# Pairing the PV quads: two quads of heads at a time in slots 0 and 8 of an attention and FFN pipeline

## What is computed

```python
def layer(x, ctx):
    q = layernorm(x) @ w_q.T                  # (8, 256, 128), 16 heads of 8
    k, v = ctx @ w_k.T, ctx @ w_v.T
    s = einsum('bhtd,bhsd->bhts', q, k) / sqrt(8)
    attn = softmax(where(mask, s, -inf), axis=-1)
    x = x + einsum('bhts,bhsd->bhtd', attn, v) @ w_o.T
    n = layernorm(x)
    h = silu(n @ (w_gate / 127).T) * (n @ (w_up / 127).T)
    return x + h @ (w_down / 127).T
```

## Time and profile before

| | us |
|---|---|
| median of 3 runs | 187.32 |
| lowest, highest | 187.08, 190.01 |
| the profiled execution | 189.59 |
| its span | 187.8 |

### The profile page before, as it was taken

The page is one execution under the profiler, slowest core; times in us unless marked ns, Lnnn a source line. Parts: engine busy times, 40 slices in busy tenths (PEclk is TensorE's granted clock), DMA queues, the critical chain, the costliest instruction groups (busy, mean ns, idle before and its releaser), DMA issues.

```text
span 187.8 us, 4293 instructions
## 1 busy us (share of the span) xinstructions
PE 168.6 (90%) x1636; PEld 105.9 (56%) x1636; DVE 133.3 (71%) x308; ACT 107.2 (57%) x226; POOL 67.0 (36%) x114
## 2 busy tenths in 40 slices
PE   5858998599996999999999999998999999997883
PEld 4648554254452556557656655754565466655863
DVE  6853897676799578968896886899689815425441
ACT  5432014657794488577867785777577577533030
POOL 6233605918427533950674085004100500310100
PEclk9996999659999699999999999999999999999999
DMA  4739797491096029405930870394000000000100
GB/s 147 261 97 183 210 179 231 134 185 24 8 245 94 3 63 213 68 0 155 173 47 12 232 133 0 93 212 67 3 30 2 3 2 28 5 28 0 31 2 28
DMA packets 17381, 17.06 MB, mean 91 GB/s; under 512 B 1520, under 2 KB 15984, under 8 KB 16688
## 3 DMA queue, kind: packets, MB, share of 16 engines
q1 hardware_dynamic: 16896, 16.12, 37.4%
q10 hardware_dynamic: 464, 0.67, 1.3%
HBM read 9.24 MB, written 7.34 MB: 88 GB/s over the span
## 4 chain that ended last, share of the span: by engine, by line
PE 54%; DVE 17%; issue 15%; POOL 6%; ACT 3%; DMA 2%; ACTq 1%; SPq 1%; POOLq 0%
PE pv_bank L336 12%; PE score_bank L276 9%; DVE neg_max L742 9%; PE pv_bank L403 5%; PE max_bank L293 4%; PE ffn_bank L389 4%; PE ffn_bank L377 3%; DMA ctx_all<-ctxT 2%; PE ffn_bank L380 2%; PE prep_bank L315 2%; PE prep_bank L307 2%; PE post_bank L365 2%; PE post_bank L352 2%; DVE stats L811 1%; PE prep_bank L311 1%
## 5 line engine op out<-in xcount | busy, mean ns | idle before, releaser
L742 DVE TENSOR_REDUCE neg_max<-max_bank 128x2 f32<-128x512 f32 x128 | 82.0, 685 | 17.9 <-PE max_bank L293 17.3
L566 ACT ACTIVATE probs<-score_bank 128x512 f32<-128x512 f32 x128 | 70.0, 597 | 20.7 <-PE score_bank L276 20.7
L293 PE MATMUL max_bank<-k_ops,q_ops 49*128 49x256 bf16 x256 | 44.0, 280 | 2.8 <-DVE neg_max L742 2.8
L276 PE MATMUL score_bank<-q_ops,k_ops 51*128 51x256 bf16 x256 | 43.7, 280 | 1.9 <-ACT probs L566 1.1
L336 PE MATMUL pv_bank<-probs,v_ops 128*32 128x256 f32 x512 | 35.2, 390 | 0.0
L276 PEld LDWEIGHTS score_bank<-q_ops,k_ops 51*128 51x128 bf16 x256 | 19.8, 95 | 22.1 <-ACT probs L566 9.9
L293 PEld LDWEIGHTS max_bank<-k_ops,q_ops 49*128 49x128 bf16 x256 | 17.4, 95 | 8.3 <-DVE neg_max L742 5.6
L990 POOL CAST max_parts<-neg_max 128x16 bf16<-128x16 f32 x14 | 2.8, 198 | 51.7 <-DVE neg_max L742 51.7
L336 PEld LDWEIGHTS pv_bank<-probs,v_ops 128*32 128x32 f32 x512 | 14.7, 110 | 11.2 <-issue 5.4
L403 PE MATMUL pv_bank<-ident_bf 128*128 128x128 bf16 x212 | 18.5, 242 | 1.9 <-POOL ident_bf L1020 1.9
L403 PEld LDWEIGHTS pv_bank<-ident_bf 128*128 128x128 bf16 x212 | 15.0, 110 | 5.9 <-issue 3.6
(11 more groups left out here) (117 smaller groups left out, 221.0 us busy)
## 6 DMA issues: line engine op xcount, KB each, us to landing
k_ops<-k_rows SPq DMA_DIRECT2D x7, 384.0 KB, 4.8
q_ops<-q_rows SPq DMA_DIRECT2D x7, 384.0 KB, 6.1
k_rows<-kq_parts SPq DMA_DIRECT2D x8, 192.0 KB, 2.1
q_rows<-kq_parts SPq DMA_DIRECT2D x8, 192.0 KB, 2.2
k_rows<-kq_parts SPq DMA_DIRECT2D x8, 128.0 KB, 2.1
q_rows<-kq_parts SPq DMA_DIRECT2D x8, 128.0 KB, 2.1
out<-y SPq DMA_DIRECT2D x8, 128.0 KB, 2.1
x_all<-x SPq DMA_DIRECT2D x1, 768.0 KB, 6.6
```

The source lines that it names most:

```text
L276: mm = pe.matmul(score_bank[k % 2][:, t * S:(t + 1) * S], rows(k_ops, b, ROWS)[:, k, t * P:(t + 1) * P], rows(q_ops, b, ROWS)[:, k, :], st ...
L293: mm = pe.matmul(max_bank[k % 2][:, t * S:(t + 1) * S], rows(q_ops, b, MAX_ROWS)[:, k, t * P:(t + 1) * P], rows(k_ops, b, MAX_ROWS)[:, k, ...
L566: act.activation(probs[:, k % RING].rearrange("p t s -> p (t s)"), score_bank[k % 2][:, :], ACT.Exp, scale=SCALE).then_inc(probs_ready, 1)
L742: dve.tensor_reduce(neg_max[:, b % 2, :, k], max_bank[k % 2][:, :].rearrange("p (t s) -> p t s", t=TT), AX.X, ALU.max, negate=True).then_i ...
```

## The change

The two quads 2 and 3 of batch b - 1 stand together in slot 0, and quads 0 and 1 of batch b in slot 8, each pair with nothing else in its slot. `turn_xn2` and `turn_max(b, 1)` go from slot 0 to slot 2, ahead of `turn_xn1` and `project_down`; `project_attn` and `turn_max(b + 1, 0)` from slot 8 to slot 10, in that order; gate and up of chunk 1 from slot 10 to slot 12, ahead of `project_v`; chunk 2 stays alone in slot 14. Step 7 is changed in its slots 0 and 2 only. ScalarE's and VectorE's orders follow: `copy_pv` stands behind exp 1, `copy_xn2_t` and `copy_max_t(b, 1)` behind exp 3, `copy_max_t(b + 1, 0)` behind exp 11, the tanh of chunk 1 behind exp 13, `residual` and `stats_of_x1` behind head_max 11, `moments_of_x1` and `eps_of_x1` behind head_max 13. No instruction is added or removed; GpSimd's and SyncE's orders stay.

```diff
@@ TensorE, the steps
                 both(b, 0)
+                if b >= 1:
+                    times_v(b - 1, 2)
+                    times_v(b - 1, 3)
+                both(b, 2)
                 if b >= 2:
                     turn_xn2(b - 2)
...
                 turn_max(b, 1, prep_bank)
-                if b >= 1:
-                    times_v(b - 1, 3)
-                both(b, 2)
...
                 times_v(b, 0)
+                times_v(b, 1)
+                both(b, 10)
+                if b >= 1:
+                    project_attn(b - 1)
                 if prep:
                     pe.wait_ge(kq_copied, b + 2)
                 else:
                     pe.wait_ge(max_t_ready, 2 * b + 2)
                 turn_max(b + 1, 0, prep_bank)
-                if b >= 1:
-                    project_attn(b - 1)
-                both(b, 10)
+                both(b, 12)
                 if b >= 2:
                     pe.wait_ge(hidden_done, CH * (b - 2) + 1)
                     project_gate_up(b - 2, 1, ffn_bank)
-                both(b, 12)
-                times_v(b, 1)
...
                     project_gate_up(b - 2, 2, ffn_bank)
-                times_v(b, 2)
 
             b = LAST
             both(b, 0)
+            times_v(b - 1, 2)
+            times_v(b - 1, 3)
+            both(b, 2)
             turn_xn2(b - 2)
             pe.wait_ge(max_t_ready, 2 * b + 1)
             turn_max(b, 1, prep_bank)
-            times_v(b - 1, 3)
-            both(b, 2)
@@ ScalarE, the steps (the same three moves stand in step 7)
                 exp(b, 0)
                 exp(b, 1)
+                if b >= 1:
+                    copy_pv(b - 1)
+                exp(b, 2)
+                exp(b, 3)
                 if b >= 2:
                     copy_xn2_t(b - 2)
                 copy_max_t(b, 1, prep_bank)
-                exp(b, 2)
-                exp(b, 3)
-                if b >= 1:
-                    copy_pv(b - 1)
-                else:
+                if b == 0:
                     place_v(2, prep_bank)
...
-                exp(b, 8)
-                exp(b, 9)
+                for k in range(8, 12):
+                    exp(b, k)
                 copy_max_t(b + 1, 0, prep_bank)
-                exp(b, 10)
-                exp(b, 11)
+                exp(b, 12)
+                exp(b, 13)
                 if b >= 2:
                     gate_tanh(b - 2, 1, ffn_bank)
-                exp(b, 12)
-                exp(b, 13)
@@ VectorE, the steps
-                head_max(b + 1, 8)
-                head_max(b + 1, 9)
+                for k in range(8, 12):
+                    head_max(b + 1, k)
                 if b >= 1:
                     residual(b - 1)
                     stats_of_x1(b - 1)
-                head_max(b + 1, 10)
-                head_max(b + 1, 11)
+                head_max(b + 1, 12)
+                head_max(b + 1, 13)
                 if b >= 1:
                     moments_of_x1(b - 1)
                     eps_of_x1(b - 1)
-                head_max(b + 1, 12)
-                head_max(b + 1, 13)
                 if b >= 2:
                     hide(b - 2, 1, ffn_bank)
```

## The result

| us | before | changed |
|---|---|---|
| median | 187.85 (4 executions) | 195.22 (4) |
| lowest, highest | 187.08, 190.01 | 194.6, 196.11 |
| the profiled execution | 189.59 | 194.6 |
| its span | 187.8 | 192.8 |
| granted clock, mean over the span | 0.964 | 0.973 |

What follows compares the result with a forecast made beforehand. TensorE's order was taken to set the time; step changes of 3.0 + 1.1 + 0.8 + 1.0 - 1.2 + 0.7 = +5.4 us on the 187.3 median gave 192.7 us, range 189.3 to 197.5.

Steps and rivals of the forecast that it cites:

- step 0: Two quads issued instead of three; -1.2 us with the saving at the pair, its new wait costing nothing.
- step 1: One quad more (+0.87) and a wait of about 1, partly absorbed by slots hanging on VectorE: +0.7 us, between 0 and +1.5.
- step 2: No project_down here; the longer slot 2 swallows about 0.4 us of waiting for maxima: +1.1 us.
- steps 3 and 4, each: Blocks of 16.51 us plus waits of 1.2, 0.2 and 0.8 give 18.7 against 17.2: +1.5 us each.
- steps 5 and 6, each: Slots 0 to 8 grow by about 1.1 us, slots 10 to 14 shrink by 0.7: +0.4 each.
- the 0.2 a step that was counted: Matmul time saved by pairing, about 0.2 us a step; 0.4 if turn_max did not count as another tiling mode.
- The wait of slot 2: turn_xn1 waits for ScalarE's copy of turn_max, queued behind exponentials: 1.2 us, in steps 1 to 4; bounds 0 to 1.5.
- The wait of slot 14: Chunk-2 gate and up waits for VectorE's hidden of chunk 1, ending 4.94 us after slot 10 starts: 0.8 us, bounds 0.5 to 1.0.
- Rival 3: VectorE takes up the moved work in time, hidden ending before 4.2 us: not slower, about 184 us; chance 0.06.
- Head 13's 0.2: In slot 12 TensorE reaches head 13 0.2 us before VectorE's maximum 11 is done.
- Nothing moved is a DMA.: No transfer moved; SP's waits for max_t come about 2 us later, with 5 us to slot 8.
- rival 1: The new waits also drop TensorE's clock, two or three more half-clock stretches of up to 1.5 us: 197 us; chance 0.16.

Runs made afterwards that it cites:

- e9: Kernel before, with identity matmuls that compute nothing of the result put in TensorE's waits of steps 0 and 1; 189.2 us, ratio 1.0027.
- changed again: The changed kernel unedited, run once more beside the kernel before on another chip; 194.96 us, ratio 1.0367 to the kernel before.
- e3: Kernel before, with only quad 2 of batch b - 1 moved from the end of slot 14 to slot 0, beside quad 3; 192.04 us, ratio 1.0146.
- e1: Changed kernel, with turn_xn1(b + 3) and its wait for the copy moved from slot 2 to slot 4; 191.64 us, ratio 1.0119 to the kernel before.
- e11: Changed kernel, with quad 2 of batches 0 and 1 back in slot 14 of their own steps; 192.69 us, ratio 1.0205 to the kernel before.
- e8: Changed kernel with the edits of e1 and e7 both; 189.66 us, ratio 1.0038 to the kernel before.
- e12: Changed kernel with the edits of e1, e7 and e11 together; 189.51 us, ratio 1.0041 to the kernel before.
- e7: Changed kernel, with quad 1 moved from slot 8 to slot 14, ahead of gate and up of chunk 2; 191.43 us, ratio 1.0091 to the kernel before.

## Why the prediction was right, point by point

**The time.** Forecast 192.7 on the median's level and 195.0 on the profiled execution's own; the profiled execution took 194.6, the median is 195.22, within the range and 2.5 above the forecast. 0.5 of that is the kernel before itself, whose median of three was 187.32 and of four 187.85; the other 2.0 is the clock in part (below). Forecast +5.4; by the steps +5.5, as follows. The spans differ by 5.0, since the changed kernel's step 0 starts 0.46 earlier: the execution before had a stretch at half clock at 14.0 us.

| part | forecast | measured |
|---|---|---|
| step 0 (both with 6.8 us at half) | -1.2 | -1.10 |
| step 1 (both with 3.4 us at half; without: e9 and changed again, +0.21) | +0.7 | +0.20 |
| step 2 | +1.1 | +1.63 |
| steps 3 and 4, each | +1.5 | +1.45 |
| steps 5 and 6, each | +0.4 | +0.42 |
| step 7 to end | +1.0 | +0.99 |
| together | +5.4 | +5.5 |

**The blocks.** A pair of quads was to take 1.87: slot 0 and slot 8 are 2.40 each against 2.41. (The forecast gave no row for the 0.87 of a second quad; the slots bear it out.) Slot 10 is 1.40 against 1.39. Slot 2 less its wait is 3.97 - 1.14 = 2.83, as worked out. Step 4 less its three waits is 18.64 - 1.14 - 0.81 - 0.19 = 16.50, against 16.51; the 0.19 in slot 12 is itself taken as what goes beyond the forecast of its blocks.

The Trainium skill, TensorEngine Tiling (Array Packing), Key Properties, has a change of the tiling mode drain TensorE. The runs agree that a change costs something, 0.13 a step for one switch less in e3; that it is a drain they don't show. Slot 10, with `turn_max` alone between two other forms, took its 1.39, so the saving is the 0.2 a step that was counted and not 0.4.

**The wait of slot 2.** Forecast 1.2 us in steps 1 to 4; measured 1.14 in step 4, four waits, all released by the copy. e1 removes it and gets 0.96 of step 4 back, 1.18 of step 2.

**The wait of slot 14.** Forecast 0.8, hidden ending at 4.94 from slot 10; measured 0.81 by slots (2.41 against 1.60) and 4.93. Five waits. Rival 3 (not slower) hung on hidden ending before 4.2 and fell with it. Head 13's 0.2 is there as well: slot 12 is 2.24 against 2.05.

**Where sizes were off.** "Step 2 ... +1.1" was 0.5 too small and "Step 1 ... +0.7" 0.5 too large. Step 1 was given "one quad more (+0.87)", and that is a miscount: quad 2 of batch 0 comes in at slot 0 and quad 2 of batch 1 leaves slot 14, so both kernels have four quads there; for steps 5 and 6 the prediction counts it so. In step 2, 0.85 of the 1.63 is the scores of slot 0 (1.39 instead of 0.54), where VectorE's maxima hold TensorE (63.89 to 65.75 above). This wait stood in no term: quad 2 had covered it from slot 14 of step 1, and e11, which puts it back there, has it gone. The two errors cancel, 1.8 forecast for steps 1 and 2 and 1.83 measured. Nothing in the working made them do so: that part of the total's agreement is luck.

**"Nothing moved is a DMA."** No line of SyncE moved, but its queue did: the 384 KB transfers stand behind the shift rows of a moved `turn_max` and are issued some 2.3 us later in the step. The margin was worked out for slot 8 and not for the next step's head 0. In the steps of the changed kernel from 2 on it cost nothing; with both waits gone it cost 0.84 in one step (e8, e12), and in e1, with one gone, 0.62 at the head of step 2.

**The clock (rival 1).** No stretch at half clock falls in steps 2 to 6 of any kernel that keeps both waits, so the rival as it was put didn't come. But the medians differ by 7.4 and 6.2 us where the steps give 5.5, and the clock accounts for a part of that. Single executions sort by it. On the chip of "changed again", executions of before took 187.66 to 188.57 us at a mean clock of 0.982 and 188.59 to 188.96 at 0.973; those of the changed kernel took 194.56 to 195.22 at 0.973 and 196.40 and 196.41 at 0.956, and none of them was above 0.974. At like clock (0.973) the difference is about 5.9. In the first comparison only the profiled execution of the kernel before has its clock on record, so its 7.4 can't be sorted. Rival 1 may have come in a mild form, in steps 0 and 1 alone. Why the changed kernel never had the higher clock in ten executions stays open. The two waits don't decide it: e11, which has both from step 2 on, reached 0.982 and e7, with one, 0.981, while e8, with neither, stayed at 0.964 or less.

## What to carry to other kernels

Where TensorE alternates with a chain of small steps on other engines, a block of matmuls is worth its length only where nothing else is waited for: before moving it, list for each slot what it covers, and for each bank who must copy it between the block that writes it and the next. Grouping matmuls of one tile form saved 0.13 us of a step for the switch removed in e3, and the waits that came where a cover was taken away were 0.8 to 1.2 us long. When a transfer hangs on a moved block, follow it to its reader, also across the step's end, and with it all that stands behind it in its queue.

## What was not expected of the hardware

- The time at half clock in steps 0 and 1 differs from one execution of the same kernel to the next: 10.2 and 17.0 us in two profiles of the kernel before, mean clocks of 0.947 to 0.991 over its executions. Matmuls that compute nothing kept it up in half of e9's executions (0.99), and step 1 got 1.5 us shorter; but at the same mean clock of 0.982 the kernel with them took 1 to 2.4 us more than the one without, and its median gained nothing (1.0027 [0.9994, 1.0061]).
- A transfer of 8 KB, issued at 92.90 us behind three others on SyncE's queue, released its reader only at 97.96, some 5 us later. The 384 KB transfer issued 1.3 us ahead of it landed at the same time, 6.5 us after its issue; the page of e8 has the two kinds of 384 KB at 4.7 and 6.1 us (medians).
